# Seven comparison matrices for a group of nodes instead of eight, and the wide layers in the step form of the narrow ones

## The reference

```python
def sage(x, src, dst, Wl, b, Wr):
    agg = segment_sum(x[src], dst, n)
    cnt = segment_sum(ones, dst, n)
    return (agg / maximum(cnt, 1)) @ Wl + b + x @ Wr

x = layernorm(x + sage(relu(sage(x, ...)), ...))             # a1, a2
x = layernorm(x + sage(relu(sage(relu(sage(x, ...)), ...)), ...))   # b1, b2, b3
```

## Time and profile before

| what | value |
|---|---|
| median of 3 runs | 5212.95 us (5212.83 to 5214.96) |
| profiled execution, its own time | 5213.1 us |
| its span, first to last instruction | 5211.5 us |
| granted PE clock, mean | 0.991 |
| PE, PEld busy | 95%, 94% of the span |
| DVE, ACT, POOL busy | 71%, 49%, 45% |
| DMA | 193 GB/s over the span |

### The profile page before, as it was taken

How to read it: one execution, slowest core, us unless ns; L and a number is a source line. 1 busy time by engine, 2 the same in 40 slices (tenths; PEclk the granted TensorE clock), 3 DMA queues, 4 the chain that set the end, 5 groups by cost and what they waited for, 6 DMA issues and landing times. The chain is left out here.

```text
span 5211.5 us, 156564 instructions
## 1 busy us (share of the span) xinstructions
PE 4970.9 (95%) x42398; PEld 4907.3 (94%) x42399; DVE 3692.6 (71%) x10002; ACT 2554.6 (49%) x7254; POOL 2342.6 (45%) x2947
## 2 busy tenths in 40 slices
PE   1899989999998999999899999999998999999999
PEld 0788889999998999999899999999998999999999
DVE  4688877888887999999666666767675555555555
ACT  0455547777774333333333333333333666666666
POOL 1788866666644444444332323222222444444441
PEclk9999999999998999999999999999999999999999
DMA  1677777888875655665555555555555766666665
GB/s 29 172 211 210 208 198 210 229 229 228 229 224 160 196 193 196 197 196 194 167 173 179 173 179 173 178 174 178 174 177 162 222 216 219 219 217 219 219 216 186
DMA packets 1247576, 1007.06 MB, mean 193 GB/s; under 512 B 70406, under 2 KB 1178275, under 8 KB 1247492
## 3 DMA queue, kind: packets, MB, share of 16 engines
q1 hardware_dynamic: 1171780, 825.23, 51.2%
q0 software_dynamic: 75712, 180.76, 11.4%
HBM read 645.58 MB, written 360.13 MB: 193 GB/s over the span
## 5 line engine op out<-in xcount | busy, mean ns | idle before, releaser
L1206 PE MATMUL f_product_b<-f_ring_b,f_onehot_b 128*128 x6272 | 997.2, 281 | 0.0
L1206 PEld LDWEIGHTS f_product_b<-f_ring_b,f_onehot_b 128*128 128x128 f32 x6272 | 856.3, 189 | 0.0
L778 PE MATMUL m_product_a<-m_ring_a,m_onehot_a 128*128 x4704 | 846.9, 291 | 0.0
L1262 ACT ACTIVATE f_ring_b<-f_e_product_b,t_rec_all 128x256 f32 (+1 forms) x784 | 329.4, 471 | 1010.0 <-PE f_e_product_b L1219 1010.0
L1200 PE MATMUL f_product_b<-b_r_all,f_t_hi_b 128*128 128x256 f32 x2352 | 723.1, 307 | 0.0
L901 DVE TENSOR_TENSOR m_onehot_b<-iota_all,t_win_all 128x512 f32<-128x512 f32 x392 | 269.6, 688 | 557.3 <-PE m_product_b L778 557.3
L1202 PE MATMUL f_product_b<-b_r_all,f_t_lo_b 128*128 128x256 f32 x2352 | 661.2, 281 | 0.0
L1201 PE MATMUL f_product_b<-b_r_all,f_t_hi_b 128*128 128x256 f32 x2352 | 659.6, 280 | 0.0
L778 PEld LDWEIGHTS m_product_a<-m_ring_a,m_onehot_a 128*128 128x128 f32 x4704 | 651.9, 192 | 0.0
L1139 POOL TENSOR_TENSOR f_held_b<-ones_all 1x1 f32<-1x1 f32 x390 | 71.5, 183 | 1243.0 <-ACT f_e_idx_b L1244 1152.6
L901 DVE TENSOR_TENSOR m_onehot_a<-iota_all,t_win_all 128x512 fp32r<-128x512 f32 (+1 forms) x784 | 536.8, 686 | 102.7 <-PE m_product_a L778 94.0
(11 more groups left out here) (197 smaller groups left out, 12292.7 us busy)
## 6 DMA issues: line engine op xcount, KB each, us to landing
g<-f_rows_out_b SPq DMA_DIRECT2D x392, 512.0 KB
f_rows_in_b<-g SPq DMA_DIRECT2D x196, 512.0 KB, 4.1
m_rows_in_b<-g SPq DMA_DIRECT2D x196, 512.0 KB
m_t_full_a<-in_x_flat_dram SPq DMA_DIRECT2D x196, 256.0 KB
h<-m_rows_out_a SPq DMA_DIRECT2D x196, 256.0 KB
m_rows_in_a<-h SPq DMA_DIRECT2D x196, 256.0 KB
m_res_in_a<-in_x_dram SPq DMA_DIRECT2D x196, 256.0 KB, 3.1
x<-m_rows_out_a SPq DMA_DIRECT2D x196, 256.0 KB
```

The source lines that it names most:

```text
L778: mm = pe.matmul(both, onehot[:, s, n, :], ring[:, bass.ds(at[n] * (C * fo), C * fo)], start=False, stop=(w == 1), skip_group_check=True)
L1206: mm = pe.matmul(to, onehot[:, s, n, :], ring[:, bass.ds(at[n] * (2 * fo) + half * fo, fo)], start=False, stop=(w == 1 and half == 1))
```

## The change

1. `window_tables` gives each node tile one window (FIRSTS = 4 a group) and each group three extra windows (EXTRAS = 3) for those node tiles whose edges go on into the next edge tile. For an extra window the table holds the edge tile, the shifted destinations and the number of the node tile (its column). WINDOWS = 7, and PLACES = 10: seven ring places and three columns. A group with more than three such node tiles counts as odd.
2. `compare` makes 4 matrices, then 3. `places` loads 10 values. `multiply` does one window for each node tile; behind node tiles 2 and 3 come the three extra windows, with a PSUM address computed from the column.
3. The wide pass takes the form of the narrow one: `phased` and `At`, D = 6, two product buffers of two banks, `s_product` once a group, both halves of `add_up` for g - 1 in step g.

```diff
+FIRSTS, EXTRAS = T, 3
+WINDOWS = FIRSTS + EXTRAS
+PLACES = WINDOWS + EXTRAS
 def window_tables(pr):
-    WB = pr.block
-    B = S // WB
+    WB = max(n for n in range(1, P + 1) if G % n == 0)
+    B = G // WB
...
-        LAST = 16 + 4 * B
+        LAST = 31 + 4 * B * T
...
+            pool.iota(turn[:, :, :, :], pattern=[[0, B], [1, EXTRAS], [0, T]], base=0, channel_multiplier=0,
+            pool.iota(inner[:, :, :, :], pattern=[[0, B], [0, EXTRAS], [1, T]], base=0, channel_multiplier=0,
...
             for b in range(B):
-                for lim, num in ((base, n_base), (end, n_end)):
-                    step(v.tensor_scalar(below[:, :], firsts[:, :], lim[:, b:b + 1], None, ALU.is_lt))
-                    step(v.tensor_reduce(num[:, b:b + 1], below[:, :], mybir.AxisListType.X, ALU.add))
+                for t in range(T):
+                    for lim, num in ((base, n_base), (end, n_end)):
+                        step(v.tensor_scalar(below[:, :], firsts[:, :], lim[:, b, t:t + 1], None, ALU.is_lt))
+                        step(v.tensor_reduce(num[:, b, t:t + 1], below[:, :], mybir.AxisListType.X, ALU.add))
...
+            for t in range(T):
+                step(v.tensor_tensor(before[:, :, t + 1], before[:, :, t], goes_on[:, :, t], ALU.add))
+            step(v.tensor_scalar(bad[:, 3, :, 0], before[:, :, T], float(EXTRAS), None, ALU.is_gt))
...
 def narrow_pass(pr, cv):
             def places(g):
-                    pr.t_slot[0:1, bass.ds(g.n(0, 2 * T), 2 * T)], engines=[mybir.EngineType.PE], min_val=0,
+                    pr.t_slot[0:1, bass.ds(g.n(0, PLACES), PLACES)], engines=[mybir.EngineType.PE], min_val=0,
...
             def multiply(g, at, u):
...
                 if u == 1:
+                    wait(pe, s_onehot, g.n(0, 2) + 2)
+                    for n in range(FIRSTS, WINDOWS):
+                        mm = pe.matmul(product[s][:, bass.ds(at[n + EXTRAS] * (C * fo), C * fo)], onehot[:, s, n, :],
+                                       ring[:, bass.ds(at[n] * (C * fo), C * fo)],
+                                       start=False, stop=True, skip_group_check=True)
                     mm.then_inc(s_product.sem, 1)
...
             def compare(g, u):
+                n0, n = ((0, FIRSTS), (FIRSTS, EXTRAS))[u]
...
 def wide_pass(pr, cv):
+    D = PHASES
...
-        e_rows = pr.sb(c, "f_e_rows", [P, 2, 2, kt * P])
+        e_rows = pr.sb(c, "f_e_rows", [P, D, 2, kt * P])
...
-        product = [pr.ps(c, f"f_product{i}") for i in range(4)]
+        product = [pr.ps(c, f"f_product{i}", (P, T * fo)) for i in range(2)]
...
+            def multiply(g, at, u):
+                s = g.slot(2)
                 if u == 0:
+                    wait(pe, s_onehot, g.n(0, 2) + 1)
+                    wait(pe, s_lo, g.n(1, kt))
+                    wait(pe, s_ringlo, min(g.off + LEAD - 2, G) if g.reg is None else g.n(LEAD - 2))
+                    wait(pe, s_sum, g.n(-1, U))
...
+                if u == 1:
+                    wait(pe, s_onehot, g.n(0, 2) + 2)
+                    for n in range(FIRSTS, WINDOWS):
+                        to = bank[:, bass.ds(at[n + EXTRAS] * fo, fo)]
                         for half in range(2):
                             mm = pe.matmul(to, onehot[:, s, n, :], ring[:, bass.ds(at[n] * (2 * fo) + half * fo, fo)],
-                                           start=False, stop=(w == 1 and half == 1))
-                mm.then_inc(s_product.sem, 1)
+                                           start=False, stop=True, skip_group_check=True)
+                    mm.then_inc(s_product.sem, 1)
...
             def step(g, p):
+                q = turned_before(g, p)
                 if p is not None:
+                    edges_lo(p)
...
                 if not is_last(g):
+                    nodes_lo(g.plus(1))
                 if has(g, 1):
+                    add_up(g.plus(-1), 0)
                 if not is_last(g):
+                    compare(g.plus(1), 0)
+                if has(g, 1):
+                    add_up(g.plus(-1), 1)
+                if not is_last(g):
+                    compare(g.plus(1), 1)
                 if q is not None:
+                    ring_lo(q)
```

More of the change, by code:

```diff
@@ L361, in _ @@
+            step(v.scalar_tensor_tensor(out=off[:, :, :], in0=tile[:, :, :], scalar=-0.5, in1=start[:, :, first],
                                         op0=ALU.mult, op1=ALU.add))
[L362 to L373, removed]
@@ L485, in wait @@
         eng.wait_ge(counter.sem, counter.at(k))
[L488 to L492, removed]
-            for n in range(3):
-                body(turn * 3 + (first + n))
-    for i in range(first + 3 * turns, end):
-        body(i)
-def steps(pr, eng, step):
-    G, L = pr.groups, LEAD // 2
-    for p in range(LEAD):
-        step(None, p, p % 2, None, p // 2)
-    for g in (0, 1):
-        step(g, g + LEAD, g, 0, L)
-    def pair(i):
-        for s in range(2):
-            step(i * 2 + s, i * 2 + (s + LEAD), s, i, i + L)
-    pairs(eng, 1, G // 2 - L - 1, pair)
-    for g in (G - LEAD - 2, G - LEAD - 1):
-        step(g, g + LEAD, g % 2, g // 2, g // 2 + L)
-    for g in range(G - LEAD, G):
-        step(g, None, g % 2, g // 2, None)
 class At:
@@ L1115, in _, with load_rows @@
-            load_rows(2, 0)
-            def step(g, s):
-                if not (isinstance(g, int) and g >= G - 3):
-                    load_rows(g + 3, 1 - s)
-                if has(g, 1):
-                    store(g - 1, 1 - s)
-            for g in (0, 1):
-                step(g, g)
-            with sp.Fori(1, G // 2 - 2) as i:
-                for s in range(2):
-                    step(i * 2 + s, s)
-            for g in range(G - 4, G):
-                step(g, g % 2)
-            store(G - 1, 1)
+            def load_rows(g):
+                wait(sp, s_turned, g.n(-1, kt))
+                sp.dma_start(rows_in[:, g.slot(2), :, :], view(h, g, kt * P)).then_inc(rows_here[g.slot(2)].sem, 16)
@@ new lines, in store, with step @@
+            def store(g):
+                wait(sp, s_sum, g.n(1, U))
+                if is_last(g):
+                    wait(sp, stored[1 - g.slot(2)], G // 2)
+                sp.dma_start(view(out, g, fo), rows_out[:, g.slot(2), :, :]).then_inc(stored[g.slot(2)].sem, 16)
+            def step(g, p):
+                if g is None:
+                    if p.off < 3:
+                        load_rows(p)
+                    return
+                if g.reg is not None or g.off + 3 < G:
+                    load_rows(g.plus(3))
+                if has(g, 1):
+                    store(g.plus(-1))
@@ L1131, in _ @@
+            phased(pr, sp, step)
+            store(At(G - 1))
             for s in range(2):
@@ new lines, in multiply @@
+                        pe.matmul(to, t_hi[:, s, k, cols], cv["r2"][:, k, 1, :], start=False, stop=False,
+                                  skip_group_check=True)
+                        pe.matmul(to, t_lo[:, s, k, cols], cv["r2"][:, k, 0, :], start=False, stop=False,
+                                  skip_group_check=True)
+                    for half in range(2):
+                        pe.matmul(to, onehot[:, s, t, :], ring[:, bass.ds(at[t] * (2 * fo) + half * fo, fo)],
+                                  start=False, stop=False, skip_group_check=True)
@@ L1236, in step @@
+                if p is not None and not is_last(p):
+                    turn_edges(p.plus(1))
                 if g is not None:
-                    multiply(g, s, at, 1)
-            turn_edges(0, 0, 0)
-            steps(pr, pe, step)
+                    multiply(g, at, 1)
+            turn_edges(At(0))
+            phased(pr, pe, step)
         @block.scalar
         def _(act):
-            def take_numbers(p, s):
-                act.activation(e_idx[:, s, :], pr.t_src[:, bass.ds(p * 2, 2)], ACT.Copy).then_inc(s_index.sem, 1)
```

352 lines of the change are left out of this document (190 added, 162 removed).

## The result

The change makes the kernel slower: 5920.9 us (median of 4 runs, 5914.5 to 5946.5) against 5213.95 us for the kernel before (4 runs beside it), a ratio of 1.136, 95% interval 1.133 to 1.140. The prediction was 5056 us with a range from 5012 to 5175.

What follows compares the result with a forecast made beforehand. PE was taken to bound every stage but a1, where POOL and the sequencer were nearer their end. From 5213.1 us, a1 0, a2 -36, b1 -37, b2 -46.8, b3 -43.6, wide ends +1.2, tables +5.5 gave 5056, range 5012 to 5175.

Steps and rivals of the forecast that it cites:

- the load's term in part 2: PE's sequencer: loading ten registers instead of eight adds 0.03 us a step, at most a quarter of the load.
- The slower rival: Sequencer, `places`: ten registers need two loads, the second costing 0.49 to 0.87 us; total 5344 us; chance 0.15.
- b2 and b3 I take in full: Window matmuls in stages b2 and b3: dropping one of eight saves its whole PE time, 46.8 and 43.6 us.
- tables: Setup ahead of a1: more pairs compared and reduced, small steps and iotas add 5.5 us in series.
- a2: Stage a2: one window matmul less a group saves 36 us, ends 10 and 44.
- b1: Stage b1: 0.19 of 0.239 us a step realised, the sequencer being near its limit; saves 37 us, ends 0 and 47.
- the addresses: Sequencer: three new PSUM address computations at 0.046 us each add 0.14 us a step.
- a sequencer that manages the same register load in a step of 3.1 us has room: Stages b2 and b3: their steps of 7.45 and 6.00 us leave the sequencer room for its added work.
- a1 would gain nothing: Stage a1: PE isn't the bound, so the change is put at 0, ends -4 and +82 us.
- POOL at 3.10 of 3.12 us: Stage a1: POOL's work and gaps fill 3.10 us of a 3.12 us step, limiting any gain to 4 us.
- 12% or more: DVE's spare time in stages b1, b2, b3 and a2, put at 12% to 47%.

Runs made afterwards that it cites:

- the table: Kernel before plus thirty kinds of register load, varied in address and number, run alone ahead of a1; ten registers from a boundary took 1.078 us.
- the packed kernel: Changed kernel with 8 words a group instead of 10, node tile number packed into its extra window's word: 5097.1 us against 5212.6, ratio 0.978.
- the static kernel: The packed kernel with the three extra windows' node tiles fixed to 0, 1 and 2: 5050.3 us against 5212.6, ratio 0.969.

## Why the prediction was wrong

**The step that failed** is the load's term in part 2, "+0.03 for two registers, upper end a quarter of the load". The upper end was +0.15 us. Measured were +0.49 us in even groups and +1.8 in odd ones, 1.75 us against 0.59 in b3. I had two points, one register at 0.49 us and eight at 0.59, and drew a line in the number. Both points were poor: in the table one register takes 0.31 us as a rule, and eight are the best case of a stepped price, two groups of four from a boundary. The trace of before couldn't show the other price, since each of its rows is 32 bytes from the last. What it could have told me is that the stride went from 32 to 40 bytes; I listed the size of the load and never its address.

**The rule of the Trainium skill.** The Trainium skill ("Runtime: NRT & Kernel Launch", "Instruction fetch mechanics") gives about 200 ns a register even in a bulk load. I set it aside because eight registers would then be 1.6 us. The table shows 0.234 us for each register that isn't in a group of four on a boundary. By this rule of the Trainium skill the two further registers would be +0.40; +0.49 was measured on a boundary. The measurements decide: for eight on a boundary the figure of the Trainium skill is too high (0.592 us instead of 1.6), for ten off a boundary it is nearly right (2.40 us instead of 2.0). The eight registers of before were the first case; the two added ones, and in odd groups all ten, are the second.

**The slower rival** had the right place, the sequencer's load in `places`, the right point of decision (less slack than the load) and the wrong mechanism. It had a second load at 0.49 to 0.87 us in every group; the load stayed one and grew by 1.8 to 2.6 us in odd groups and, outside b2, by 0.1 to 0.5 in even ones. Its sum of 5344 was far short.

**"b2 and b3 I take in full"** failed with it. Their slack was real, but small. In b1 the load started 1.9 us ahead of the matmul behind it, and a load of 1.08 us is hidden in b3, where the first of the two loads above costs PE nothing. But a load of 2.4 to 3.3 us is longer than the sequencer's lead in every stage. So the stages that were purely PE-bound lost time too, b3 42 us and b2 175.

**What held**, read from the packed kernel, whose load is in number and boundary that of before:

| term | predicted, us | packed kernel, us |
|---|---|---|
| tables | +5.5 | +5.1 |
| a1 | 0 | +21.0 |
| a2 | -36 | -35.1 |
| b1 | -37 | -46.6 |
| b2 | -46.8 | -16.5 |
| b3 | -43.6 | -43.8 |

It has the whole of the wide form too. Its total is -116 (spans 5211.5 and 5095.5) against -157: a1 and b2 fall short by 21 and 30 us, and b1 gives 10 more than the sequencer was thought to leave. The tables measured +5.7 in after itself.

In a1 and b2 unpacking and computed addresses are not hidden (an address computation takes 0.079 us where a PSUM address comes with it, instead of 0.046, and up to 0.146 with unpacking). The prediction took 0.14 us a step for the addresses and called b2's room enough for them; the static kernel, which has neither, is at -0.2 in a1 and -33.2 in b2. By the starts of PE's instructions b2's missing 30 us are 0.09 us a step in front of the first transpose (17 us) and 0.05 us by which the transposes take longer (10 us); in the static kernel the same two are 4 and 7 us. So "a sequencer that manages the same register load in a step of 3.1 us has room" was wrong for b2 in the packed kernel too, by a small sum.

That a1 would gain nothing came true in the static kernel, but the reason given, POOL at 3.10 of 3.12 us, isn't borne out. That figure is work plus gaps, which fill a stretch whatever bounds it, and in the static kernel POOL ran ahead at 3.02 us a step while PE waited for its sequencer. What holds a1 there at 3.10 us was not tried.

One reading was off without consequence: DVE has 9% to spare in b1 (819.01 of 900 us), not 12% or more.

**Left open.** In b2 the load takes 0.4 to 0.9 us more than in the table under the new form of the wide pass (packed 1.07, static 1.47, eight words of before 1.45, ten 1.9, twelve 1.67), but with before's rows of 8 words not under the old one (0.67), and not in b1. The depth of the gathers isn't it, nor are the computed addresses, which static lacks. The form alone doesn't decide it either: under the old form with rows of 10 words, the odd groups' loads took 2.81 us in b1, where the table has 1.93, and 2.03 in b2. In a1 and a2 the same eight words took 0.95 and 0.89 us before and 0.61 packed. Nothing that I found in the rows goes with it in all stages. The same may lie behind the 2.7 to 3.3 us of after's odd groups, where the table has 2.4.

## What to carry to other kernels

When a table is read into registers, its rows should start on a 16-byte boundary and the number of registers be a multiple of four. Padding the rows cost nothing that shows in the setup (it ends at 139.3 us with rows of 12 words, 139.8 with 16, 140.1 with 10), and rows of 12 words with all twelve loaded beat rows of 16 with ten loaded by 89 us here. Cost a load by address and number, not by number alone, and ask of every changed row length what it does to the alignment of the rows behind it. Look at minimum and maximum of a group before its mean: two alternating values are the sign of an address that steps past a boundary.

## What was unexpected in the hardware

- The price of a register load on PE's sequencer: 0.256 us for each four registers if the first word is on a 16-byte boundary of the table, 0.234 us for every other single one, so 16 registers take 1.10 us from a boundary and 3.80 from two words past it.
- A longer load can be charged twice where it leaves PE idle: in a1 of after the granted clock fell to 0.53 behind a gap of 2.69 us, and its mean over the stage to 0.90. It isn't every gap: in a1 of the kernel before with rows of 10 words PE stood still 94 times, 1.6 us in the median (102 times and 2.2 us in after), and the clock over that stage is 0.98.
- One chip ran the kernel before in 5338 us, the others in 5213 to 5214; in a kernel with before's stages that was profiled there, a1 took 728 us instead of 628, and the other stages were near their usual times. Each ratio above is against the kernel before on the same chip.
